# Moving the ternary quantisation of a weight into the last batch of a kernel's first half, and reordering the transfers at the change of halves

## The chip, the cores and the metric

The kernel runs on one core of one Trainium2 chip. The metric is the device time of one execution in microseconds (us); the median over several executions counts. The engines are called TensorE (PE in the profile; PEld is its weight load), VectorE (DVE), ScalarE (ACT), GpSimd (POOL) and SyncE (SP, which here issues every DMA transfer, in the order of its program).

## What is computed

The input x has 8 batches of 1024 tokens by 512 channels, fp32. Each token row is layer-normalised to xn, and the output is x + attention(xn) + ffn(xn).

```python
# attention, per batch
xm  = x * time_mix + shifted(x) * (1 - time_mix)
k   = exp(min(xm @ Wk.T, 60)); v = xm @ Wv.T; r = xm @ Wr.T
# per channel, along the tokens: a decaying sum of k*v and of k (a scan)
rwkv = sigmoid(r) * wkv / sum_k
out_attention = rwkv @ Wo.T
# feed-forward
xn2   = layernorm(x) * ln_gamma + ln_beta
beta  = mean(|weight|)                       # one number for the whole weight
w_q   = clip(round(weight / (beta + eps)), -1, 1)     # ternary
gamma = max(|xn2|)                           # one number over all 8 batches
y     = (clip(xn2 * 128 / gamma) @ w_q) * (gamma * beta / 128)
```

Because gamma is a maximum over all batches, the feed-forward product can't start before every batch has been normalised once. The ternary weight w_q depends on the weight alone.

## The kernel before

**Two halves.** Batches 0 to 3 form the first half (phase A in the code), batches 4 to 7 the second (phase B). In phase A a batch b gets its attention, and at the same time the feed-forward inputs of batch b and of batch b + 4 are normalised, transposed on TensorE, evacuated by ScalarE, searched for their absolute maximum by VectorE and stored to DRAM (`ffn_input`). The attention result of a phase-A batch is stored to `attn_scratch`. In phase B a batch b gets its attention, its own feed-forward product and that of batch b - 4, whose stored attention result is read back into the tile `parked`.

**The groups.** A batch has two token tiles of 512 tokens (0 and 1), and each tile has four chunks of 128 channels: eight chunks c. Every chunk has three projections, k, v and r, so a batch runs over 24 groups g = 3c + m (m = 0, 1, 2 for k, v, r). Each group on TensorE is 12 matmuls (a split of fp32 into a high and a low part, three products for each of four input chunks), `project`, L467. In phase A each group also has one transposition slot n = g (`slot`, L454), in the order of `SLOT_KINDS` (L44): 0 to 3 ffn_own0, 4 to 7 ffn_other0, 8 to 11 mix_own1, 12 to 15 ffn_own1, 16 to 19 ffn_other1, 20 to 23 mix_next0. All slots share one PSUM bank: the transposes of slot n wait until ScalarE has evacuated slot n - 1 (L456). The attention output of tile 0, 48 matmuls, runs after group 12, and that of tile 1 after group 23 (`attn_out`, L488). In phase B the feed-forward products (32 matmuls each, `ffn_out`, L508) stand behind groups 4, 9, 16 and 21.

**The order on each engine is written out by hand.** Every engine works through its own program in order and waits on semaphores; a wait holds everything behind it. For the last batch of phase A (b = 3) the steps that matter are these.

- VectorE, `batch` (L979), at g = 12 (m = 0, c = 4): `clamp_k`, `denominator`, `rwkv`, `rwkv_lo` of chunk 3, then `tile_stats("other1")` (L1018), then `add_out("attn0")` (L1019, four adds from the PSUM banks to the x tile). At g = 13: the absolute maximum of slot 13 (L859) and `recurrence` of chunk 4 (L918: the product k*v at L923, which frees the bank for the next v projection, two scans, and the sum L940). At g = 14 and 15 the maxima of slots 14 and 15, at g = 16 that of slot 16 and `tile_stats("next0")`. After the last group come `ternary_sum` (L896, the sum of |weight| by partition), `quantise` (L901), `scales` (L1050) and `add_out("attn1")`.
- ScalarE, `batch` (L717): at g = 14 it evacuates slot 14, normalises two of the four 128-token blocks of the tile `other` and takes `exp_r(4)`; at g = 15 it evacuates slot 15 (L590), then `exp_k(5)` and `ln_sums(4)` (L696, which needs VectorE's sum of chunk 4); at g = 16 it evacuates slot 16, once plain into `parked` (L589) and once scaled (L590). After the last group it waits for VectorE's rounding and writes the four chunks of `w_ternary` (L756 to L759).
- GpSimd, `batch_a` (L1159): statistics arithmetic and half of each normalisation. `other(b, "other1")` (L1167, the helper is at L1138) starts when VectorE's statistics of `other1` are ready (L1144) and ends with the row `mix_over_ffn_stat` (L1156); then comes `mix_scale` for next0. After the batch come the sum over partitions (L1198, `partition_all_reduce`), for which VectorE waits in `quantise` (L902), and the maximum over partitions (L1200), for which VectorE waits in `scales` (L1052).
- SyncE, `batch_a` (L328) with `is_last`: at the end it waits for all stores from `parked`, loads the weight into `parked` (L354), then the feed-forward input of other0 in four chunks into the tile `other` (L359), stores x[1] to scratch (L361), loads the next x[1] (L363); behind that come the mix input (L422, a 1 MB load into `normed` and a broadcast row), the load of `parked` (L424) and, at the head of `batch_b`, the four chunks of own0 (L375, the issue is at L371).

In phase B, ScalarE evacuates a chunk of `other` once it has landed (L594) and so frees it for the next load; its evacuation of own0 chunk 0 stands at g = 4, in front of `exp_r(1)` and what follows. The tile `parked` is the same memory as `PLAIN` (L115): slots 4 to 7 and 16 to 19 of phase A write it, and the weight is loaded into it.

Of the kernel before, what the change touches and what calls it, by code (L numbers as in the profile page):

```python
# [24 lines left out]
ALU = mybir.AluOpType  # L25
ACT = mybir.ActivationFunctionType
AX = mybir.AxisListType

P = 128
# [3 lines left out]
FFN_EPS = 1e-5  # L33
# [29 lines left out]
def mixed_decay_kernel(nc, x, constants, weights, Wf, out):  # L63
# [19 lines left out]
    with ExitStack() as ctx:  # L83
# [208 lines left out]
        def _(sp):  # L292
# [35 lines left out]
            def batch_a(b, is_last=False):  # L328
# [4 lines left out]
                store_ffn_input(b, 7)  # L333
                store_row(b, 0)
                store_ffn_input(b, 12)

# [12 lines left out]
                if is_last:  # L349

                    for r in range(RING):
                        sp.wait_ge(s_fst[r], 16 * 2 * HALF)
                        sp.wait_ge(s_plain[r], 16 * 2 * HALF)
                    sp.dma_start(ZB[:, :, :], Wf.rearrange("(i p) c -> p i c", p=P)).then_inc(s_w[4], 16)  # L354
                    for t in range(2):
                        sp.wait_ge(s_inv[t], 16 * HALF + 16)
                    sp.wait_ge(pe_t, slots_before(b, "A", first_slot("ffn_other1") + CH))
                    for ch in range(CH):
                        sp.dma_start(ZA[:, ch, :], ffn_in[0, 0, ch]).then_inc(s_fld[ch], 16)  # L359
                sp.wait_ge(dve_out, BANKS + bank_use(b, "A", "attn1") + Q)  # L360
                sp.dma_start(scratch_t[b, 1], X[1][:, :, :]).then_inc(s_xst[1], 16)  # L361
                sp.wait_ge(s_xst[1], 16 * b + 16)
                sp.dma_start(X[1][:, :, :], x_t[b + 1, 1]).then_inc(s_x[1], 16)  # L363

            def load_ffn_input(b, what, ch):
# [7 lines left out]
            def batch_b(b, is_last=False):  # L373
                for ch in range(CH):
                    load_ffn_input(b, "own0", ch)  # L375
                sp.wait_ge(dve_out, BANKS + bank_use(b, "B", "other0") + Q)
# [43 lines left out]

            sp.wait_ge(pe_t, slots_before(HALF - 1, "A", len(SLOTS)))
            load_mix_input(HALF, 1)  # L422
            sp.wait_ge(act_q, CH)
            sp.dma_start(ZB[:, :, :], scratch_t[0, 0]).then_inc(s_park, 16)  # L424
            for b in range(HALF, B - 1):
# [131 lines left out]
        def _(act):  # L557
# [145 lines left out]
            def rwkv_hi(b, ph, c):  # L703
# [11 lines left out]
                nc.scalar.activation(RH[:, j, :], KV[:, c % 2, 1, :], ACT.Copy).then_inc(act_rh, 1)  # L715

            def batch(b, ph, is_last=False, last_a=False):  # L717
                last = None
                for g in range(GROUPS):
# [21 lines left out]
                    elif m == 2:  # L741
                        if c and c != CH:
                            rwkv_hi(b, ph, c - 1)
                        if g == ATTN0_AFTER - 1:
                            high_part(b, ph, last)
                            last = None
                            if ph == "A":
                                normalise(b, ph, "ffn_own1")
                        exp_r(b, c)
                ln_sums(b, CHUNKS - 1)  # L750
                if last is not None:
                    high_part(b, ph, last)
                quotient(b, CHUNKS - 1)
                rwkv_hi(b, ph, CHUNKS - 1)
                if last_a:
                    act.wait_ge(dve_q, 3)  # L756
                    for i in range(CH):
                        nc.scalar.activation(WQ[:, i, :], ZB[:, i, :], ACT.Sign,
                                             bias=round_c[:, :]).then_inc(act_q, 1)  # L759
                elif ph == "A":  # L760
                    normalise(b + 1, ph, "ffn_own0")
# [12 lines left out]
        def _(dve):  # L774
# [126 lines left out]
            def quantise():  # L901
                dve.wait_ge(pool_sum, 1)  # L902
                V.tensor_scalar(sc[:, 2:3], sc[:, 1:2], 1.0 / (C * C), None, ALU.mult).then_inc(dve_s, 1)
                dve.wait_ge(dve_s, 2)
                V.tensor_scalar(sc[:, 3:4], sc[:, 2:3], FFN_EPS, None, ALU.add).then_inc(dve_s, 1)
                dve.wait_ge(dve_s, 3)
                V.reciprocal(sc[:, 4:5], sc[:, 3:4]).then_inc(dve_q, 1)
# [71 lines left out]
            def batch(b, ph, is_last=False, last_a=False):  # L979
                last = None  # L980
                for g in range(GROUPS):
# [28 lines left out]
                    if m == 0:  # L1010
                        clamp_k(b, c)
                        if c:
                            denominator(b, c - 1)
                            if c == CH:
                                rwkv(b, c - 1)
                                rwkv_lo(b, c - 1)
                                if ph == "A":
                                    tile_stats(b, ph, "other1", is_last)  # L1018
                                add_out(b, ph, "attn0")  # L1019
                    elif m == 1:  # L1020
# [13 lines left out]
                if last_a:  # L1034
                    ternary_sum()
                    quantise()
                    scales()
# [34 lines left out]
        def _(pool):  # L1072
# [86 lines left out]
            def batch_a(b, is_last=False):  # L1159
# [6 lines left out]
                normalise(XN, X[1], own[:, 1], 1, pool_xn)  # L1166
                other(b, "other1")  # L1167
                mix_scale(*mix_call(b, "A", "next0"), own[:, 0])
                pool.wait_ge(pe_t, slots_before(b, "A", first_slot("ffn_own1") + CH))
# [26 lines left out]
            batch_a(HALF - 1, is_last=True)  # L1196
            pool.wait_ge(dve_q, 1)
            G.partition_all_reduce(sc[:, 1:2], sc[:, 0:1], P, bass.bass_isa.ReduceOp.add).then_inc(pool_sum, 1)  # L1198
            pool.wait_ge(dve_s, 1)
            G.partition_all_reduce(sc[:, 6:7], sc[:, 5:6], P, bass.bass_isa.ReduceOp.max).then_inc(pool_max, 1)  # L1200
# [36 lines left out]
```

## Time and profile before

| quantity | value |
|---|---|
| time, median of 3 runs | 922.42 us (918.77, 922.57, 922.42) |
| time of the profiled execution | 919.68 us |
| its span | 917.9 us |
| mean granted TensorE clock | 0.992 |
| TensorE busy | 880.4 us, 96% |
| VectorE busy | 761.5 us, 83% |
| ScalarE busy | 509.4 us, 56% |
| GpSimd busy | 188.1 us, 20% |
| phase B starts on TensorE | 440.9 us from the start of the span |

The profiled execution takes 1.8 us more than its span. The times below are microseconds from the span's start. In a timeline a row gives start, duration, engine, source line, operation, tile written and tiles read, the shape, and how many instructions it merges; what stands in brackets is the engine's idle time before it and who ended it. Durations of neighbours on one engine overlap a little, so the step from one to the next is shorter than a duration: a matmul row shows about 0.4 us and the next begins 0.23 us later.

### The profile page before, as it was taken

The page shows a single profiled execution, that of the slowest core. Times are in us where ns is not written, and L with a number is a line of the kernel's source. Part 1 is how long each engine was busy: PE and PEld are TensorE (multiplying, and loading weights), DVE is VectorE, ACT ScalarE, POOL GpSimd, SP SyncE. Part 2 cuts the span into 40 slices and gives each one's busy share as a digit, 9 for nine tenths or more (in the row PEclk, how much of TensorE's full clock was granted, in tenths as well). Part 3 has the DMA queues.
Part 4 walks back from the last instruction along what each step waited for, and adds up shares of the span by engine and source line. Part 5 has one row for each costly group of instructions (what it writes and reads, how often), then busy time and mean ns, then how long its engine had stood idle before and what let it go on. Part 6 is the DMA issues. An engine that isn't in the chain of part 4 may idle for free.

```text
span 917.9 us, 12736 instructions
## 1 busy us (share of the span) xinstructions
PE 880.4 (96%) x3984; PEld 714.3 (78%) x3984; DVE 761.5 (83%) x1282; ACT 509.4 (56%) x830; POOL 188.1 (20%) x242
## 2 busy tenths in 40 slices
PE   2989999999999999999989999999999999999998
PEld 2768777787878777787867888888888888888886
DVE  5998988889798988889768887887878978789684
ACT  3674757657574757657445363554545544455441
POOL 5442333143242333140010020100201102011000
PEclk9999999999999999999999999999999999999999
DMA  8222415042422415043425443253332532334211
GB/s 275 105 81 80 150 41 186 15 149 69 149 80 77 152 46 181 14 151 112 154 97 185 138 144 111 80 192 137 110 115 107 194 137 92 104 137 138 92 47 46
DMA packets 59841, 107.13 MB, mean 117 GB/s; under 512 B 7712, under 2 KB 7712, under 8 KB 59808
## 3 DMA queue, kind: packets, MB, share of 16 engines
q1 hardware_dynamic: 59808, 106.73, 34.2%
q8 instruction: 16, 0.26, 0.1%
q14 instruction: 17, 0.14, 0.0%
HBM read 64.76 MB, written 41.96 MB: 116 GB/s over the span
## 4 chain that ended last, share of the span: by engine, by line
PE 63%; DVE 18%; issue 9%; ACT 4%; DMA 4%; POOL 1%; SPq 0%; DVEq 0%; ACTq 0%; POOLq 0%
PE kvr L483 12%; PE kvr L485 12%; PE kvr L484 12%; PE out_banks L519 6%; PE out_banks L521 6%; PE out_banks L498 5%; PE out_banks L501 5%; PE out_banks L500 5%; DVE scans L933 4%; DVE bn_stats L796 3%; PE transposed L441 2%; DMA other<-ffn_input 1%; DVE rwkv_lo L953 1%; DVE k_and_kv L923 1%; DVE k_and_kv L949 1%
## 5 line engine op out<-in xcount | busy, mean ns | idle before, releaser
L483 PE MATMUL kvr<-xm_hi,wk_hi 128*128 128x512 f32 x256 | 104.4, 408 | 7.2 <-DVE xm_lo L876 4.6
L1186 POOL TENSOR_TENSOR evacuated<-normed,mix_over_ffn_row 128x512 f32<-128x512 f32 x28 | 36.3, 1296 | 360.0 <-DVE ffn_lo L876 360.0
L483 PE MATMUL kvr<-xm_hi,wv_hi 128*128 128x512 f32 x256 | 102.9, 402 | 1.6 <-DVE k_and_kv L923 1.1
L483 PE MATMUL kvr<-xm_hi,wr_hi 128*128 128x512 f32 x256 | 103.3, 404 | 0.0
L498 PE MATMUL out_banks<-wo_hi,rwkv_hi 128*128 128x512 f32 x256 | 101.9, 398 | 0.5 <-DVE rwkv_lo L953 0.5
L485 PE MATMUL kvr<-xm_hi,wk_lo 128*128 128x512 f32 x256 | 101.5, 396 | 0.0
L501 PE MATMUL out_banks<-wo_hi,rwkv_lo 128*128 128x512 f32 x256 | 101.3, 396 | 0.0
L500 PE MATMUL out_banks<-wo_lo,rwkv_hi 128*128 128x512 f32 x256 | 101.2, 395 | 0.0
L519 PE MATMUL out_banks<-w_ternary,ffn_hi 128*128 128x512 f32 x256 | 100.0, 390 | 1.3 <-DVE ffn_lo L876 1.3
L484 PE MATMUL kvr<-xm_lo,wk_hi 128*128 128x512 f32 x256 | 100.9, 394 | 0.0
L485 PE MATMUL kvr<-xm_hi,wr_lo 128*128 128x512 f32 x256 | 100.4, 392 | 0.0
L485 PE MATMUL kvr<-xm_hi,wv_lo 128*128 128x512 f32 x256 | 100.1, 391 | 0.0
L484 PE MATMUL kvr<-xm_lo,wr_hi 128*128 128x512 f32 x256 | 100.0, 391 | 0.0
L521 PE MATMUL out_banks<-w_ternary,ffn_lo 128*128 128x512 f32 x256 | 99.7, 390 | 0.0
L484 PE MATMUL kvr<-xm_lo,wv_hi 128*128 128x512 f32 x256 | 99.7, 389 | 0.0
L689 ACT ACTIVATE gate<-kvr 128x512 f32<-128x512 f32 x64 | 37.8, 591 | 88.8 <-PE kvr L485 88.8
L940 DVE SCALAR_TENSOR_TENSOR k_and_kv<-k_and_kv,constants,scans 128x1024 f32<-128x1024 f32 x64 | 83.4, 1303 | 1.1
L933 DVE TENSOR_TENSOR_SCAN scans<-constants,state,k_and_kv 128x512 f32<-128x512 f32 x64 | 79.7, 1287 | 0.0
L590 ACT ACTIVATE evacuated<-transposed,constants 128x512 f32<-128x512 f32 x64 | 49.6, 774 | 50.9 <-PE transposed L441 47.3
L933 DVE TENSOR_TENSOR_SCAN scans<-constants,k_and_kv 128x512 f32<-128x512 f32 x64 | 75.1, 1215 | 0.0
L627 ACT ACTIVATE ffn_hi<-evacuated 128x512 fp32r<-128x512 f32 x64 | 39.9, 623 | 50.7 <-DVE evacuated L862 48.4
L876 DVE TENSOR_TENSOR ffn_lo<-evacuated,ffn_hi 128x512 fp32r<-128x512 f32 x64 | 44.0, 687 | 25.4 <-ACT ffn_hi L627 25.1
(125 smaller groups left out, 1910.7 us busy)
## 6 DMA issues: line engine op xcount, KB each, us to landing
other<-ffn_input SPq DMA_DIRECT2D x64, 256.0 KB, 5.4
x<-in_x SPq DMA_DIRECT2D x15, 1024.0 KB, 5.7
other<-in_x SPq DMA_DIRECT2D x8, 1024.0 KB, 5.7
ffn_input<-evacuated SPq DMA_DIRECT2D x32, 256.0 KB, 4.6
ffn_input<-parked SPq DMA_DIRECT2D x32, 256.0 KB, 2.1
attn_scratch<-x SPq DMA_DIRECT2D x8, 1024.0 KB, 4.3
parked<-attn_scratch SPq DMA_DIRECT2D x8, 1024.0 KB, 7.1
out<-parked SPq DMA_DIRECT2D x8, 1024.0 KB, 5.2
```

Of the source, the lines that this page charges most:

```text
L483: nc.tensor.matmul(KVR[:, m, :], hi, XH[t][:, ch, :], start=(ch == 0), stop=False)
L484: nc.tensor.matmul(KVR[:, m, :], hi, XL[t][:, ch, :], start=False, stop=False)
L485: last = nc.tensor.matmul(KVR[:, m, :], lo, XH[t][:, ch, :], start=False, stop=(ch == CH - 1))
L498: nc.tensor.matmul(OUT[:, q, :], hi, WH["o"][:, j, :], start=(j == 0 and ph == "A"), stop=False)
L500: nc.tensor.matmul(OUT[:, q, :], hi, WL["o"][:, j, :], start=False, stop=False)
L501: last = nc.tensor.matmul(OUT[:, q, :], lo, WH["o"][:, j, :], start=False, stop=(j == CH - 1))
L519: nc.tensor.matmul(OUT[:, q, :], AH[:, ch, q * P:(q + 1) * P], WQ[:, ch, :], start=(ch == 0), stop=False)
L521: last = nc.tensor.matmul(OUT[:, q, :], AL[:, ch, q * P:(q + 1) * P], WQ[:, ch, :], start=False, stop=(not own_tile and ch == CH - 1))
L590: nc.scalar.activation(U[:, r, :], bank, ACT.Identity, bias=bet[:, ch:ch + 1], scale=gam[:, ch:ch + 1]).then_inc(act_u, 1)
L876: V.tensor_tensor(lo, U[:, n % RING, :], hi.bitcast(F32), ALU.subtract).then_inc(dve_lo, 1)
L933: last = V.tensor_tensor_scan(S[:, i, 1:TILE + 1], dec, kv[:, i, :], 0.0 if t == 0 else state[:, j, i:i + 1], ALU.mult, ALU.add)
L940: V.scalar_tensor_tensor(kv, kv, first[:, j:j + 1], S[:, :, 0:TILE], ALU.mult, ALU.add).then_inc(dve_sum, 1)
```

## The change

The load of the feed-forward weight moves from the end of SyncE's last phase-A batch to just behind `store_row(b, 0)`. `ternary_sum` and `quantise` on VectorE move from the end of that batch to g = 12, between `tile_stats("other1")` and `add_out("attn0")`; `scales` stays. GpSimd's sum over partitions moves to just behind `other(b, "other1")`; its maximum over partitions stays behind the batch. ScalarE's four ternary chunks move to the ends of g = 14 and g = 15, two each. On SyncE the load of `parked` goes ahead of other0's chunks, the mix input ahead of the store of x[1], and own0's four chunks ahead of the load of the next x[1]. The counts of the semaphore `dve_s` are renumbered to the new order.

```diff
--- before.py
+++ after.py
@@ -332,6 +332,11 @@
                 sp.dma_start(ZA[:, :, :], x_t[b + HALF, 1]).then_inc(s_oth, 16)
                 store_ffn_input(b, 7)
                 store_row(b, 0)
+                if is_last:
+
+                    for ch in range(CH):
+                        sp.wait_ge(s_plain[ch], 16 * (2 * b + 1))
+                    sp.dma_start(ZB[:, :, :], Wf.rearrange("(i p) c -> p i c", p=P)).then_inc(s_w[4], 16)
                 store_ffn_input(b, 12)
 
                 sp.wait_ge(dve_out, BANKS + bank_use(b, "A", "attn0") + Q)
@@ -351,16 +356,26 @@
                     for r in range(RING):
                         sp.wait_ge(s_fst[r], 16 * 2 * HALF)
                         sp.wait_ge(s_plain[r], 16 * 2 * HALF)
-                    sp.dma_start(ZB[:, :, :], Wf.rearrange("(i p) c -> p i c", p=P)).then_inc(s_w[4], 16)
+                    load_parked()
                     for t in range(2):
                         sp.wait_ge(s_inv[t], 16 * HALF + 16)
                     sp.wait_ge(pe_t, slots_before(b, "A", first_slot("ffn_other1") + CH))
                     for ch in range(CH):
                         sp.dma_start(ZA[:, ch, :], ffn_in[0, 0, ch]).then_inc(s_fld[ch], 16)
+                    sp.wait_ge(pe_t, slots_before(b, "A", len(SLOTS)))
+                    load_mix_input(HALF, 1)
                 sp.wait_ge(dve_out, BANKS + bank_use(b, "A", "attn1") + Q)
                 sp.dma_start(scratch_t[b, 1], X[1][:, :, :]).then_inc(s_xst[1], 16)
+                if is_last:
+
+                    for ch in range(CH):
+                        load_ffn_input(HALF, "own0", ch)
                 sp.wait_ge(s_xst[1], 16 * b + 16)
                 sp.dma_start(X[1][:, :, :], x_t[b + 1, 1]).then_inc(s_x[1], 16)
+
+            def load_parked():
+                sp.wait_ge(act_q, CH)
+                sp.dma_start(ZB[:, :, :], scratch_t[0, 0]).then_inc(s_park, 16)
 
             def load_ffn_input(b, what, ch):
 
@@ -371,8 +386,9 @@
                 sp.dma_start(ZA[:, ch, :], ffn_in[bb, int(what[-1]), ch]).then_inc(s_fld[ch], 16)
 
             def batch_b(b, is_last=False):
-                for ch in range(CH):
-                    load_ffn_input(b, "own0", ch)
+                if b > HALF:
+                    for ch in range(CH):
+                        load_ffn_input(b, "own0", ch)
                 sp.wait_ge(dve_out, BANKS + bank_use(b, "B", "other0") + Q)
                 sp.dma_start(out_t[b - HALF, 0], ZB[:, :, :]).then_inc(s_parkst, 16)
                 for ch in range(CH):
@@ -418,10 +434,6 @@
                 batch_a(b)
             batch_a(HALF - 1, is_last=True)
 
-            sp.wait_ge(pe_t, slots_before(HALF - 1, "A", len(SLOTS)))
-            load_mix_input(HALF, 1)
-            sp.wait_ge(act_q, CH)
-            sp.dma_start(ZB[:, :, :], scratch_t[0, 0]).then_inc(s_park, 16)
             for b in range(HALF, B - 1):
                 batch_b(b)
             batch_b(B - 1, is_last=True)
@@ -713,6 +725,14 @@
                     if ph == "B":
                         act.wait_ge(pe_out, bank_use(b, ph, "other0"))
                 nc.scalar.activation(RH[:, j, :], KV[:, c % 2, 1, :], ACT.Copy).then_inc(act_rh, 1)
+
+            TERNARY_AT = {14: (0, 1), 15: (2, 3)}
+
+            def ternary(chunks):
+
+                act.wait_ge(dve_q, 3)
+                for i in chunks:
+                    nc.scalar.activation(WQ[:, i, :], ZB[:, i, :], ACT.Sign, bias=round_c[:, :]).then_inc(act_q, 1)
 
             def batch(b, ph, is_last=False, last_a=False):
                 last = None
@@ -747,17 +767,14 @@
                             if ph == "A":
                                 normalise(b, ph, "ffn_own1")
                         exp_r(b, c)
+                    if last_a and g in TERNARY_AT:
+                        ternary(TERNARY_AT[g])
                 ln_sums(b, CHUNKS - 1)
                 if last is not None:
                     high_part(b, ph, last)
                 quotient(b, CHUNKS - 1)
                 rwkv_hi(b, ph, CHUNKS - 1)
-                if last_a:
-                    act.wait_ge(dve_q, 3)
-                    for i in range(CH):
-                        nc.scalar.activation(WQ[:, i, :], ZB[:, i, :], ACT.Sign,
-                                             bias=round_c[:, :]).then_inc(act_q, 1)
-                elif ph == "A":
+                if ph == "A" and not last_a:
                     normalise(b + 1, ph, "ffn_own0")
 
             with act.Fori(0, HALF - 1) as b:
@@ -901,9 +918,9 @@
             def quantise():
                 dve.wait_ge(pool_sum, 1)
                 V.tensor_scalar(sc[:, 2:3], sc[:, 1:2], 1.0 / (C * C), None, ALU.mult).then_inc(dve_s, 1)
+                dve.wait_ge(dve_s, 1)
+                V.tensor_scalar(sc[:, 3:4], sc[:, 2:3], FFN_EPS, None, ALU.add).then_inc(dve_s, 1)
                 dve.wait_ge(dve_s, 2)
-                V.tensor_scalar(sc[:, 3:4], sc[:, 2:3], FFN_EPS, None, ALU.add).then_inc(dve_s, 1)
-                dve.wait_ge(dve_s, 3)
                 V.reciprocal(sc[:, 4:5], sc[:, 3:4]).then_inc(dve_q, 1)
                 dve.wait_ge(dve_q, 2)
                 V.tensor_scalar(ZB[:, :, :], ZB[:, :, :], sc[:, 4:5], ROUND, ALU.mult, ALU.add).then_inc(dve_q, 1)
@@ -1016,6 +1033,9 @@
                                 rwkv_lo(b, c - 1)
                                 if ph == "A":
                                     tile_stats(b, ph, "other1", is_last)
+                                if last_a:
+                                    ternary_sum()
+                                    quantise()
                                 add_out(b, ph, "attn0")
                     elif m == 1:
                         if c and c != CH:
@@ -1032,8 +1052,6 @@
                     tile_stats(b + 1, ph, "other0", is_last)
                     largest(b)
                 if last_a:
-                    ternary_sum()
-                    quantise()
                     scales()
                 add_out(b, ph, "attn1")
 
@@ -1165,6 +1183,9 @@
                 pool.wait_ge(pe_t, slots_before(b, "A", first_slot("mix_own1") + CH))
                 normalise(XN, X[1], own[:, 1], 1, pool_xn)
                 other(b, "other1")
+                if is_last:
+                    pool.wait_ge(dve_q, 1)
+                    G.partition_all_reduce(sc[:, 1:2], sc[:, 0:1], P, bass.bass_isa.ReduceOp.add).then_inc(pool_sum, 1)
                 mix_scale(*mix_call(b, "A", "next0"), own[:, 0])
                 pool.wait_ge(pe_t, slots_before(b, "A", first_slot("ffn_own1") + CH))
                 normalise(XN, X[0], own[:, 0], 0, pool_xn)
@@ -1194,9 +1215,7 @@
             with pool.Fori(0, HALF - 1) as b:
                 batch_a(b)
             batch_a(HALF - 1, is_last=True)
-            pool.wait_ge(dve_q, 1)
-            G.partition_all_reduce(sc[:, 1:2], sc[:, 0:1], P, bass.bass_isa.ReduceOp.add).then_inc(pool_sum, 1)
-            pool.wait_ge(dve_s, 1)
+            pool.wait_ge(dve_s, 3)
             G.partition_all_reduce(sc[:, 6:7], sc[:, 5:6], P, bass.bass_isa.ReduceOp.max).then_inc(pool_max, 1)
             with pool.Fori(HALF, B - 1) as b:
                 batch_b(b)
```

## Rows read from the trace of the kernel before

**Rows 1.** the page, part 1: busy time, share of the span, instructions

```profile
PE 880.4 (96%) x3984; PEld 714.3 (78%) x3984; DVE 761.5 (83%) x1282; ACT 509.4 (56%) x830; POOL 188.1 (20%) x242
```

**Rows 2.** timeline of TensorE: start, duration (us), instruction, tiles, count

```profile
440.93 0.39 PE L483 MATMUL kvr<-xm_hi,wk_hi 128*128 128x512 f32 x1
...
497.49 0.39 PE L498 MATMUL out_banks<-wo_hi,rwkv_hi 128*128 128x512 f32 x1
...
564.32 0.39 PE L483 MATMUL kvr<-xm_hi,wk_hi 128*128 128x512 f32 x1
...
614.19 0.39 PE L498 MATMUL out_banks<-wo_hi,rwkv_hi 128*128 128x512 f32 x1
```

**Rows 3.** timeline of TensorE, 476 us; in brackets idle time and who ended it

```profile
476.00 0.50 PE L483 MATMUL kvr<-xm_hi,wk_hi 128*128 128x512 f32 x1 [2.63 <-ACT k_and_kv L685]
```

**Rows 4.** busy time by stretch; PEclk is the granted TensorE clock, 1.00 full

```profile
core 0: us, PE busy (x) PEld busy (x) DVE busy (x) ACT busy (x) POOL busy (x), PEclk, DMA share, GB/s
...
477.40:480.70 3.30, 3.30 (x10) 2.53 (x9) 3.30 (x7) 2.35 (x4) 1.29 (x1) 0.50 0.00 0
```

**Rows 5.** timeline around the change of halves: SyncE's queue, then ScalarE

```profile
452.10 3.26 SPq L371 DMA_DIRECT2D other<-ffn_input  x4
...
464.85 0.81 ACT L599 ACTIVATE evacuated<-other,beta_beta,gamma_beta 128x512 f32<-128x512 f32 x1 [8.21 <-DMA other<-ffn_input]
```

**Rows 6.** timeline of VectorE, end of the last batch of the first half

```profile
437.89 2.28 DVE L898 TENSOR_REDUCE scalars<-parked 128x1 f32<-128x2048 f32 x1
440.75 0.15 DVE L903 TENSOR_SCALAR scalars<-scalars 128x1 f32<-128x1 f32 x1 [0.57 <-POOL scalars L1198]
...
442.53 0.15 DVE L1053 SCALAR_TENSOR_TENSOR scalars<-scalars 128x1 f32<-128x1 f32 x1
```

**Rows 7.** timeline of ScalarE, the ternary weights

```profile
442.65 2.56 ACT L758 ACTIVATE w_ternary<-parked,minus_round 128x512 fp32r<-128x512 f32 x4 [5.39 <-DVE parked L909]
```

**Rows 8.** timeline of GpSimd, last batch of the first half

```profile
392.43 0.20 POOL L1146 TENSOR_SCALAR stat_work<-mean_var 128x4 f32<-128x4 f32 x1 [14.28 <-DVE mean_var L801]
...
400.14 0.39 POOL L1156 TENSOR_TENSOR mix_over_ffn_stat<-stat_work 128x4 f32<-128x4 f32 x1 [0.18 <-POOLq L1157]
...
440.31 0.40 POOL L1198 PARTITION_ALL_REDUCE scalars<-scalars  x1 [25.42 <-DVE scalars L898]
```

**Rows 9.** instructions of lines 1079, 1198, 1186: count, min/median/max ns, first and last start

```profile
L1079 POOLq MODIFY_POOL_CONFIG  x2: 11/11/11, 1.3 to 1.3; - x2
L1079 POOL TENSOR_SCALAR_AFFINE_SELECT ident<-ident x1: 292/292/292, 1.4 to 1.4; 128x128 f32<-128x128 f32 x1
...
L1198 POOLq MODIFY_POOL_CONFIG  x2: 8/8/8, 414.8 to 414.9; - x2
...
L1186 POOL TENSOR_TENSOR evacuated<-normed,mix_over_ffn_row x28: 1286/1297/1304, 472.5 to 836.0; 128x512 f32<-128x512 f32 x28
L1186 POOLq MODIFY_POOL_CONFIG  x6: 11/11/11, 460.2 to 668.7; - x6
```

**Rows 10.** timeline of VectorE, middle of the last batch of the first half

```profile
392.15 2.45 DVE L971 TENSOR_TENSOR x<-x,out_banks 128x512 f32<-128x512 f32 x4
...
396.02 0.69 DVE L923 TENSOR_TENSOR k_and_kv<-k_and_kv,kvr 128x512 f32<-128x512 f32 x1 [0.83 <-PE kvr L485]
...
400.39 0.68 DVE L859 TENSOR_REDUCE absmax<-evacuated 128x1 f32<-128x512 f32 x1
...
404.82 0.69 DVE L859 TENSOR_REDUCE absmax<-evacuated 128x1 f32<-128x512 f32 x1 [0.46 <-ACT evacuated L590]
```

**Rows 11.** timeline of ScalarE, the same stretch

```profile
400.47 0.76 ACT L590 ACTIVATE evacuated<-transposed,constants 128x512 f32<-128x512 f32 x1
...
402.92 0.71 ACT L696 ACTIVATE k_and_kv<-k_and_kv,k_eps 128x512 f32<-128x512 f32 x1
403.53 0.59 ACT L589 ACTIVATE parked<-transposed 128x512 f32<-128x512 f32 x1
```

**Rows 12.** timeline of TensorE, the same stretch

```profile
402.22 0.60 PE L441 MATMUL transposed<-ident,other 128*128 128x128 f32 x4
```

## Prediction

> **What bounds the kernel now.** I read the page first: TensorE is busy 96% of the span [rows 1], so only time in which it stands still or runs slowly can be won, and any new standstill is lost. Next I compared two like stretches of TensorE's timeline. From the first k projection of a phase-B batch to its first attention-output matmul the work is the same in every batch. In the first phase-B batch it takes 497.49 - 440.93 = 56.56 us, in a later one 614.19 - 564.32 = 49.87 us [rows 2]. So the change of halves costs TensorE 6.7 us, and that is all that can be won there. Of this, 2.63 us is one wait for ScalarE's exp of k [rows 3]. From 477.4 to 480.7 us the granted clock was 0.50, that is 1.2 instead of 2.4 GHz, where it had been full before that wait [rows 4]. The reader should look for what ended last behind this. The four loads of own0 were issued from 452.10 us on, behind five transfers of x, the mix input and `parked`. ScalarE stood 8.21 us for the first of them, until 464.85 [rows 5], with exp_r(1) and all later work of its program behind it.
>
> The ternary work itself costs TensorE almost nothing before: VectorE spends 442.53 - 437.89 = 4.6 us on sum and rounding [rows 6] and ScalarE 2.56 us [rows 7], but TensorE already runs projections of phase B, from 440.93 us on, without a gap.
>
> **The change part by part.**
>
> *The transfers.* The own0 loads now wait only for other0's evacuations and go out beside a single 1 MB store. I expect the first to land well before ScalarE asks for it, and take the full 6.7 us as gain; the lower end is 0, if another wait takes the place. The weight load moves to a quiet place: `parked` is free once other0's four stores have landed, SyncE's next item comes many microseconds later, and VectorE asks for the weight only at 392 us. `parked` from scratch and the mix input go out earlier, each well ahead of its reader. The load of x[1] falls behind four own0 issues, but x[1] is first touched at the end of that batch. I cost all of these at 0.
>
> *The sum over partitions.* This is where I expect the loss. At g = 12 VectorE now sums |weight| behind the statistics of other1. The statistics end where the adds of attn0 began, 392.15 us [rows 10], and the sum takes 2.28 us [rows 6], so it is done at 394.4. Then VectorE waits for GpSimd. But GpSimd has just been released by these same statistics and works through `other1` from 392.43 to 400.14 + 0.39 = 400.53 us [rows 8]; its sum over partitions stands behind that.
>
> *The configuration of GpSimd.* Before its sum over partitions GpSimd runs two MODIFY_POOL_CONFIG, at 414.8 us, and before the first ordinary multiply of phase B again, at 460.2 [rows 9]. In the kernel before, both had room behind them: the first 25.42 us of idleness [rows 8], the second 472.5 - 460.2 = 12.3 us [rows 9]. In the changed kernel the pair stands directly between 400.53 and a sum for which VectorE waits. Call its price L. Lower end: 0, since at the start of the kernel an operation followed its pair within 0.1 us [rows 9], though that pair need not have changed anything. Upper end: 12.3 us, since the multiply at 472.5 was released by VectorE and ran at once. No row decides between them; neither end is a real switch with nothing to hide it, so I take the middle, L = 6.1 us.
>
> The Trainium skill (GPSIMD Engine Reference, section Instruction dispatch) says that the first call into a freshly loaded kernel pays a load of about 6 us (5.95 us, counted from MODIFY_POOL_CONFIG) that the profile doesn't show. That rule speaks against this change; no row here shows such a load uncovered. With 5.95 instead of 6.1 us the sum would be 0.15 us less.
>
> *The sum for VectorE.* Sum over partitions and its signal: 0.57 us [rows 6], so VectorE goes on at 400.53 + 0.57 + L = 401.1 + L. Scalars and rounding take 442.53 - 440.75 = 1.78 us [rows 6]: 402.9 + L. The four adds (about 2.4) and one maximum (about 0.6) [rows 10] come next, so k*v of chunk 4 starts at 405.9 + L, against 396.02 before [rows 10].
>
> *The sum for ScalarE.* From that product to the maximum of slot 14, directly behind the chunk's sum, is 400.39 - 396.02 = 4.37 us [rows 10]: ln_sums(4) can start at 410.3 + L. It takes 403.53 - 402.92 = 0.6 us [rows 11]. Then two ternary chunks, half of 2.56 us = 1.3 [rows 7]. Then the two evacuations of slot 16, after which VectorE's maximum of slot 16 started 404.82 - 403.53 = 1.3 us later [rows 10, 11]. That maximum starts at 413.5 + L, against 404.82: a lag of **8.7 + L** us, 14.8 with L = 6.1.
>
> *What of it reaches TensorE.* All of it, I think. Slot 16 is transposed only when slot 15 is evacuated, which ScalarE does behind the first two ternary chunks, at 402.9 + L + 1.3 + 0.7 = 404.9 + L. TensorE was there at 402.22 [rows 12], so it stands 2.7 + L = 8.8 us. Then the v projection waits for k*v until 406.6 + L, and slot 17 for the evacuation of slot 16. Behind that, VectorE's order runs nearly gapless to the end of the batch and TensorE is close behind it, so neither catches up, and in phase B TensorE has no gaps in which lost time could be hidden. A long standstill may lower the clock again: in the one case shown, TensorE worked at half speed for 3.3 us behind a wait [rows 3, 4] and so lost half of that, 1.6 us. I take one such stretch, with ends at 0 (it falls into the standstill) and 3.2 (two).
>
> *At the end of the half.* VectorE and ScalarE are rid of 4.6 and 2.6 us there. TensorE didn't wait for them, so this gives nothing beyond the 6.7 us. GpSimd's switch back to ordinary operations starts at 401.1 + L and is first asked for after the maximum of slot 16, at 413.5 + L plus statistics: over 12 us of cover. The third switch, ahead of the maximum over partitions, has the 25 us that cover it now [rows 8].
>
> **The sum.** 14.8 + 1.6 - 6.7 = **+9.7 us**. Against the profiled execution (919.68 us: 917.9 of span and 1.8 around it) that gives 929.4. The median of the runs shown stands 2.7 above that execution, but the mean of all four times shown is 920.9; I take that as the base: **930.6 us**. A measurement of this kernel can tell about 0.5%, 4.6 us, from no change.
>
> **The rivals.**
>
> *A, the switch costs nothing* (L = 0, the code is resident). For it: the pair at the start that cost 0.1 us; against it: the pair's being there. Even so VectorE waits from 394.4 to 401.1 us for GpSimd's `other1`, and the sum is 8.7 + 0 to 1.6 - 6.7 = +2 to +3.6: about 923.5, no change that can be told. Chance 0.14.
>
> *B, the switch costs as much as the trace leaves room for*, 12.3 us: 21.0 + 1.6 - 6.7 = +15.9, 936.8. Chance 0.07.
>
> *C, the change of halves is not mended*: own0 is on time, but something behind it (the exp chain, x[1], the mix input) holds TensorE as long. Then 14.8 + 1.6 = +16.4, 937.3. Against it: in later phase-B batches the same code has no gap [rows 2]. Chance 0.10.
>
> *D, faster.* VectorE's wait for GpSimd stays off TensorE's path, because TensorE has transposes and projections queued ahead until slot 16. The only gain of 6.7 us is then left: 914.2. It decides at slot 16: TensorE is there at 402.22 us, so the rounding would have to be done by about 400.2, which is before GpSimd has even finished `other1`. So it also needs GpSimd to be much quicker beside an idle VectorE. Chance 0.04.
>
> **How the numbers follow.** My forecast has 0.65. The predicted time is that of the forecast, 930.6. The range reaches from rival A's 923.5 to L of about 12 or rival C, 937.5: **923.5 to 937.5**; it holds the forecast's own spread (clock 0 to 3.2 us, base 2 us either way, GpSimd perhaps 1 us quicker). Faster by over 0.5%: 0.04 (D). Within 0.5%: A and the lowest part of the forecast, 0.16. Slower by over 0.5%: 0.80.
>
> **What would show each step.** In the changed kernel's profile:
> - GpSimd: MODIFY_POOL_CONFIG near 400.6 us, and the sum over partitions L later; if it starts within 1 us, A is right. If it starts near 407, the forecast is.
> - VectorE: a wait for GpSimd of 6.7 + L, near 13 us, in front of the line that scales the sum.
> - ScalarE: a wait of several us in front of the first ternary chunk; TensorE: waits for ScalarE's evacuation ahead of slot 16 (about 9 us) and slot 17, and one for k*v between them, with a granted clock of 0.50 in a stretch near them.
> - The first k projection of phase B starts at 440.93 + 16.4, about 457 us, and the stretch from it to the first attention output is 49.9 us, without ScalarE's wait for own0.
>
> I am wrong if the last A batch shows waits of TensorE under 5 us in total, or if the stretch of the first phase-B batch stays above 53 us.

## The result, and the profile after

| | before | changed |
|---|---|---|
| median | 920.67 us (918.77 to 922.57, 4 runs) | 934.33 us (933.76 to 934.40, 4 runs) |
| profiled execution | 919.68 us, span 917.9 | 934.32 us, span 932.5 |

The ratio is 1.0152, with a 95% interval of 1.013 to 1.0175: slower by 1.5%, 13.7 us. The forecast was 930.6 with a range of 923.5 to 937.5.

The page's head and its first part say only that the same work lies in a longer span (compare [rows 1]):

```profile
span 932.5 us, 12742 instructions
...
PE 883.2 (95%) x3984; PEld 717.0 (77%) x3984; DVE 761.2 (82%) x1282; ACT 509.6 (55%) x830; POOL 181.7 (19%) x242
```

Two stretches of TensorE's timeline say where the time went. I time the first from the v projection of chunk 4 in the last batch of the first half (right behind the point where the ternary work now sits) to the first k projection of the second half: 440.93 - 392.99 = 47.94 us before, 462.25 - 393.47 = 68.78 after, so **20.8 us lost**. The second runs from there to the first attention output of the second half: 56.56 us before [rows 2], and after the change, by TensorE's timeline,

```profile
462.25 0.39 PE L495 MATMUL kvr<-xm_hi,wk_hi 128*128 128x512 f32 x1
```

```profile
512.13 0.39 PE L510 MATMUL out_banks<-wo_hi,rwkv_hi 128*128 128x512 f32 x1
```

512.13 - 462.25 = 49.88 us, which is the length of a later batch, so **6.7 us won**. The difference, 14.2, and the 0.5 us by which this execution was already later at the v projection make the 14.6 us between the spans.

**GpSimd** (instructions by line: count, min/median/max ns, first and last start). Line 1188 is the moved sum over partitions, line 1111 the first ordinary operation of `mix_scale`:

```profile
L1188 POOLq MODIFY_POOL_CONFIG  x2: 11/11/11, 399.7 to 399.8; - x2
L1188 POOL PARTITION_ALL_REDUCE scalars<-scalars x1: 401/401/401, 405.4 to 405.4; - x1
```

```profile
L1111 POOLq MODIFY_POOL_CONFIG  x2: 11/11/11, 423.7 to 423.7; - x2
```

From the pair at 399.8 us to the sum at 405.4 there are 5.7 us in which GpSimd had nothing to wait for: VectorE's part had been ready since 394.9. The second pair stands at 423.7, not behind the sum. GpSimd's timeline shows what came of it:

```profile
430.46 0.19 POOL L1111 TENSOR_SCALAR stat_work<-mean_var 128x4 f32<-128x4 f32 x1 [24.62 <-issue]
...
432.33 0.20 POOL L1114 TENSOR_TENSOR own_stats<-stat_work,own_stats 128x4 f32<-128x4 f32 x1 [0.18 <-POOL own_stats L1113]
```

The arithmetic for next0 starts 6.7 us behind the pair. In the kernel before, the same line (there L1093) started 0.2 us behind the statistics:

```profile
408.62 0.43 POOL L1093 TENSOR_SCALAR stat_work<-mean_var 128x4 f32<-128x4 f32 x1 [8.09 <-DVE mean_var L801]
```

**VectorE** (timeline; compare [rows 10]):

```profile
392.62 2.25 DVE L915 TENSOR_REDUCE scalars<-parked 128x1 f32<-128x2048 f32 x1
405.87 0.15 DVE L920 TENSOR_SCALAR scalars<-scalars 128x1 f32<-128x1 f32 x1 [11.00 <-POOL scalars L1188]
...
407.65 2.47 DVE L988 TENSOR_TENSOR x<-x,out_banks 128x512 f32<-128x512 f32 x4
...
410.64 0.68 DVE L940 TENSOR_TENSOR k_and_kv<-k_and_kv,kvr 128x512 f32<-128x512 f32 x1
...
418.24 0.69 DVE L876 TENSOR_REDUCE absmax<-evacuated 128x1 f32<-128x512 f32 x1 [1.04 <-ACT evacuated L602]
420.44 2.47 DVE L813 BATCH_NORM_STATS2 bn_stats<-x 128x6 f32<-128x512 f32 x4 [1.52 <-DMA x<-in_x]
```

The reader should see one wait of 11.00 us for GpSimd at 405.87 (forecast 6.7 + 5.7 = 12.4), then the chain of the prediction: adds at 407.65 (forecast 402.9 + 5.7 = 408.6), k*v at 410.64 (411.6), the maximum of slot 16 at 418.24 (419.2), each about 1 us early. GpSimd's `other1` was quicker than in the kernel before: it ran from 392.90 to 399.80, 6.9 us, against 8.1 us in [rows 8]. A small wait that I had not listed follows at 420.44: 1.52 us for the next x[0]. Its load stands behind the store of x[0], and that behind the delayed adds. In the kernel before, these statistics followed without a gap at 405.42.

**ScalarE** (timeline; compare [rows 11]):

```profile
407.77 1.33 ACT L735 ACTIVATE w_ternary<-parked,minus_round 128x512 fp32r<-128x512 f32 x2 [6.71 <-DVE parked L926]
409.01 0.76 ACT L602 ACTIVATE evacuated<-transposed,constants 128x512 f32<-128x512 f32 x1
...
415.74 1.32 ACT L735 ACTIVATE w_ternary<-parked,minus_round 128x512 fp32r<-128x512 f32 x2
...
424.06 0.63 ACT L727 ACTIVATE rwkv_hi<-k_and_kv 128x512 fp32r<-128x512 f32 x1 [3.84 <-DVE k_and_kv L966]
...
432.56 1.52 ACT L654 ACTIVATE normed<-x,own_stats 128x512 f32<-128x512 f32 x2 [5.48 <-POOL own_stats L1114]
```

It waits 6.71 us for the rounding, 3.84 us for a product of VectorE that stands behind the late statistics of next0, and 5.48 us for `own_stats`, which is the second switch.

**TensorE** (timeline, the waits ahead of slots 16, 17, 19 and 20; what ended them is ScalarE's evacuation each time):

```profile
410.01 1.09 PE L453 MATMUL transposed<-ident,other 128*128 128x128 f32 x4 [7.16 <-ACT evacuated L602]
```

```profile
418.26 0.66 PE L453 MATMUL transposed<-ident,other 128*128 128x128 f32 x4 [1.57 <-ACT evacuated L602]
```

```profile
427.14 0.66 PE L453 MATMUL transposed<-ident,other 128*128 128x128 f32 x4 [2.29 <-ACT evacuated L602]
```

```profile
436.56 1.08 PE L453 MATMUL transposed<-ident,normed 128*128 128x128 f32 x4 [6.00 <-ACT evacuated L602]
```

Each names ScalarE. Behind ScalarE stand the rounding (slot 16), VectorE's sum of the chunk (17), its product behind the statistics of next0 (19) and GpSimd's switch (20). The granted clock fell during the two long ones (busy time by stretch):

```profile
core 0: us, PE busy (x) PEld busy (x) DVE busy (x) ACT busy (x) POOL busy (x), PEclk, DMA share, GB/s
406.20:416.20 10.00, 5.82 (x15) 4.51 (x16) 9.89 (x16) 3.57 (x6) 0.00 (x0) 0.50 0.42 136
433.50:440.10 6.60, 3.54 (x11) 2.99 (x12) 4.87 (x8) 5.12 (x9) 0.88 (x2) 0.50 0.17 41
442.00:450.00 8.00, 8.00 (x41) 6.60 (x40) 6.56 (x17) 7.36 (x14) 0.43 (x1) 1.00 0.60 98
```

There were two stretches at 0.50 (1.2 GHz). In the first TensorE stood still nearly half the time and its one projection would have had to wait for slot 17 anyway. In the second, the projection behind slot 20 took 4.3 us (437.30 to 441.63 in the timeline) where its like takes 3.0. Behind the wait of 2.29 us at slot 19 the projection ran at full speed.

**SyncE at the change of halves** (timeline; compare [rows 5]):

```profile
463.16 0.37 SPq L368 DMA_DIRECT2D attn_scratch<-x  x1
463.58 11.51 SPq L386 DMA_DIRECT2D other<-ffn_input  x4
475.13 0.43 SPq L374 DMA_DIRECT2D x<-in_x  x1
```

own0's first chunk goes out 0.4 us behind the store, ahead of x[1]. ScalarE never waits for it.

### The profile page after: what moved, and what is told of

Its sections match the earlier page's. It is cut to its first block, busy times and chain, and to the rows that moved or that the text cites. A ratio compares the mean times of both kernels' runs of the same rounds, so it can differ in the third digit from the quotient of the medians.

```text
span 932.5 us, 12742 instructions
## 1 busy us (share of the span) xinstructions
PE 883.2 (95%) x3984; PEld 717.0 (77%) x3984; DVE 761.2 (82%) x1282; ACT 509.6 (55%) x830; POOL 181.7 (19%) x242
## 4 chain that ended last, share of the span: by engine, by line
PE 68%; DVE 16%; issue 7%; ACT 5%; DMA 2%; POOL 1%; SPq 0%; DVEq 0%; ACTq 0%; POOLq 0%
PE kvr L495 13%; PE kvr L497 13%; PE kvr L496 13%; PE out_banks L533 6%; PE out_banks L531 6%; PE out_banks L510 5%; PE out_banks L513 5%; PE out_banks L512 5%; DVE scans L950 3%; DVE bn_stats L813 3%; PE transposed L453 2%; DVE rwkv_lo L970 1%; DVE k_and_kv L940 1%; DVE absmax L876 1%; DVE k_and_kv L966 1%
## 5 line engine op out<-in xcount | busy, mean ns | idle before, releaser
L453 PE MATMUL transposed<-ident,normed 128*128 128x128 f32 x260 | 41.5, 284 | 25.9 <-ACT evacuated L602 11.6
```

The source lines that it names most:

```text
L453: last = nc.tensor.transpose(bank[:, q * P:(q + 1) * P], src[:, q, ch * P:(ch + 1) * P], ident[:, :])
```

## Experiments

The two stretches of TensorE's timeline, in us, and the medians. The kernel before ran beside each group on the same chip: 919.90 us beside e1 to e4, 919.76 beside e5 to e7.

| kernel | v of chunk 4 to second half | first batch to attention output | median | ratio to before (95%) |
|---|---|---|---|---|
| before | 47.94 | 56.56 | | |
| changed | 68.78 | 49.88 | 934.33 | 1.0152 (1.013 to 1.0175) |
| e1 transfers alone | 47.95 | 49.90 | 912.82 | 0.9923 (0.991 to 0.9935) |
| e2 ternary alone | 68.77 | 51.20 | 934.98 | 1.0167 (1.0152 to 1.0182) |
| e3 switch back early | 62.42 | 49.87 | 927.38 | 1.0085 (1.0068 to 1.0103) |
| e4 no switch | 56.66 | 49.88 | 921.62 | 1.0022 (1.0013 to 1.0032) |
| e5 no switch, ahead of other1 | 51.85 | 49.88 | 916.70 | 0.9965 (0.9953 to 0.9976) |
| e6 own0 alone ahead | 47.95 | 54.06 | 917.93 | 0.9974 (0.9964 to 0.9985) |
| e7 sum one group earlier | 49.19 | 49.88 | 917.06 | 0.9969 (0.9959 to 0.9979) |

**e1, the transfers alone**, on the kernel before:

```diff
                 sp.dma_start(scratch_t[b, 1], X[1][:, :, :]).then_inc(s_xst[1], 16)
+                if is_last:
+                    load_ffn_input(HALF, "own0", 0)
+                    sp.wait_ge(act_q, CH)
+                    sp.dma_start(ZB[:, :, :], scratch_t[0, 0]).then_inc(s_park, 16)
+                    for ch in range(1, CH):
+                        load_ffn_input(HALF, "own0", ch)
                 sp.wait_ge(s_xst[1], 16 * b + 16)
```

The mix input goes ahead of this store, as in the change.

> The kernel before with the new order of transfers alone: own0's chunks ahead of the next x[1], mix input ahead of the store of x[1], parked between own0's first and second chunk (it must wait for the ternary chunks, which stay at the end of the half). Theory 1 (late own0 loads cost the 6.7 us at the change of halves, the ternary work at the end of the half costs nothing): 6 to 7 us less than before, about 914, and 49.9 us from the first k projection of the second half to its first attention output. Rival (the ternary work at the end of the half is what makes the first batch of the second half slow): no change, about 920.7, and that stretch stays at 56 us.

Measured: 912.82 us, 7.1 less than before, and 49.90 us for the first batch. SyncE's timeline:

```profile
446.79 0.37 SPq L363 DMA_DIRECT2D attn_scratch<-x  x1
447.20 0.51 SPq L379 DMA_DIRECT2D other<-ffn_input  x1
447.75 1.01 SPq L367 DMA_DIRECT2D parked<-attn_scratch  x1
448.98 7.57 SPq L379 DMA_DIRECT2D other<-ffn_input  x3
456.59 0.43 SPq L371 DMA_DIRECT2D x<-in_x  x1
```

The whole gain at the change of halves is there with the ternary work still at the end of the half. So the transfers are enough for it. This kernel is faster than both the kernel before and the changed one.

**e2, the ternary work alone**: the changed kernel with the old order of `parked`, mix input, x[1] and own0.

> The changed kernel with the old order of transfers at the change of halves (the early weight load stays, it is needed). Theory 1: the whole lag of the last batch of the first half, 21.3 us, and the late own0 loads again: 20 to 22 us more than before, about 941 to 943. Rival (the gain comes from taking the ternary work away from the end of the half): like the changed kernel, about 934.

Measured: 934.98 us. The lag is that of the changed kernel, 68.77, but the first batch lost only 51.20 - 49.88 = 1.3 us, not 6.7. My expectation missed by 6 to 8 us, and the rival's number was right. ScalarE's wait for own0 is still there, but shorter than the 8.21 us of [rows 5]:

```profile
480.00 0.82 ACT L606 ACTIVATE evacuated<-other,beta_beta,gamma_beta 128x512 f32<-128x512 f32 x1 [4.46 <-DMA other<-ffn_input]
```

SyncE's timeline shows why. First the store of x[1] in the kernel before, then e2 from that store on:

```profile
445.61 0.37 SPq L361 DMA_DIRECT2D attn_scratch<-x  x1
```

```profile
462.35 0.37 SPq L365 DMA_DIRECT2D attn_scratch<-x  x1
...
468.85 5.42 SPq L379 DMA_DIRECT2D other<-ffn_input  x4
```

The store of x[1] was issued 462.35 - 461.44 = 0.9 us after the first k projection of the second half, against 445.61 - 440.93 = 4.7 us in the kernel before, because VectorE's adds of attn1 no longer stand behind the ternary work. The four transfers behind it, and own0 behind those, move with it: own0 is issued 468.85 - 461.44 = 7.4 us after that projection, against 452.10 - 440.93 = 11.2 [rows 5]. So own0 was late for two reasons in a row. Either move alone takes most of the 6.7 us (the transfers 6.7, the ternary work 5.4), and the two don't add up.

**e3, the switch back at once**:

```diff
                     G.partition_all_reduce(sc[:, 1:2], sc[:, 0:1], P, ...).then_inc(pool_sum, 1)
+                    G.tensor_scalar(touch[:, :], half_pos[:, 0:1], 1.0, 0.0, ALU.mult, ALU.add)
```

> The changed kernel with one small ordinary GpSimd operation on one number per partition straight behind the sum over partitions, so that GpSimd switches back to ordinary operations there and not behind its wait for the statistics of next0. Theory 1 (the switch back costs 6.7 us of TensorE's time because it stands behind that wait): 6 to 8 us less than the changed kernel, about 927, and ScalarE's wait of 5.5 us for own_stats is gone. Rival (the lag is the ternary work itself in a full stretch, the switch back lies beside it): no change, about 934.

Measured: 927.38, 6.9 us less than the changed kernel. The second pair now runs right behind the sum over partitions (instructions of the line of `touch`):

```profile
L1190 POOLq MODIFY_POOL_CONFIG  x2: 83/83/83, 405.2 to 405.3; - x2
```

In its waits from 400 to 470 us (engine, tile and line that waited, and whom for: total us, times, longest) the second switch lies under VectorE's own work:

```profile
DVE scalars L921 <- POOL scalars L1189: 10.8, 1, 10.8
...
POOL touch L1190 <- issue: 7.0, 1, 7.0
...
POOL scalars L1189 <- issue: 5.4, 1, 5.4
```

Nobody waits for `touch`, and 68.78 - 62.42 = **6.4 us** of TensorE's time came back. That is standstill alone: TensorE's waits between slots 16 and 20 add up to 17.4 us in the changed kernel and to 11.1 here. A stretch at half speed is still there, behind the 2.40 us wait at slot 19; the projection that starts with this row needed 4.3 us:

```profile
427.48 0.78 PE L496 MATMUL kvr<-xm_hi,wv_hi 128*128 128x512 f32 x1
```

**e4, no switch**: the sum over partitions is replaced by an ordinary operation in the same place. The kernel leaves that sum out and so works with a wrong beta; its other instructions and waits are those of the changed kernel.

```diff
-                    G.partition_all_reduce(sc[:, 1:2], sc[:, 0:1], P, ...).then_inc(pool_sum, 1)
+                    G.tensor_scalar(sc[:, 1:2], sc[:, 0:1], 128.0, 0.0, ALU.mult, ALU.add).then_inc(pool_sum, 1)
```

> The changed kernel with the sum over partitions left out: an ordinary GpSimd operation multiplies each partition's own sum by 128 instead, so that there is no switch in the last batch of the first half. All other instructions and waits stay. Theory 1 (both switches are exposed, 5.7 and 6.7 us, with a half-speed stretch behind them): 12 to 14 us less than the changed kernel, about 921 to 922; what is left of the lag is GpSimd's other1 and the ternary work itself, 8 us, against a gain of 6.7. Rival (the ternary work in a full stretch is the loss): 930 or more.

Measured: 921.62. The waits from 390 to 430 us:

```profile
DVE scalars L920 <- POOL scalars L1188: 5.1, 1, 5.1
...
PE transposed L453 <- ACT evacuated L602: 4.8, 4, 2.3
```

Against e3, another 62.42 - 56.66 = **5.8 us**: the first switch. What stays is 56.66 - 47.94 = 8.7 us. Of this, 5.2 us are longer waits of TensorE (6.3 us in the stretch against 1.1 before); the rest is time at half speed, which the trace shows from 403.9 to 407.2 and from 410.7 to 414.2 us. VectorE still waits 5.1 us for GpSimd, now for `other1` alone.

**e5, as e4, ahead of `other1`**:

```diff
-                other(b, "other1")
                 if is_last:
                     pool.wait_ge(dve_q, 1)
                     G.tensor_scalar(sc[:, 1:2], sc[:, 0:1], 128.0, ...).then_inc(pool_sum, 1)
+                other(b, "other1")
```

> As e4 (the sum over partitions left out, each partition's own sum times 128 instead, so no switch), and this operation stands ahead of other1 in GpSimd's program, not behind it. Theory 1 (of the 8.7 us of lag that e4 kept, GpSimd's other1, 6 us after VectorE's sum, is the larger part, and the ternary work itself costs 2 to 3 us): 4 to 6 us less than e4, 916 to 917.5, and about 50.5 us instead of 56.7 from the v projection of chunk 4 to the first k projection of the second half. Rival (VectorE and ScalarE are so full there that their 4 and 2.6 us of ternary work are the lag, wherever the sum comes from): within 2 us of e4, 920 to 921.6.

Measured: 916.70, and 51.85 us, so 56.66 - 51.85 = **4.8 us** for `other1` and 51.85 - 47.94 = **3.9 us** for the ternary work. That last part was more than the 2 to 3 expected: 2.5 us are longer waits, and about 1.4 us come from one projection at half speed, from 416.32 us on, behind the longest of them. TensorE's waits for ScalarE's evacuations are down to (390 to 450 us)

```profile
PE transposed L453 <- ACT evacuated L602: 3.7, 3, 2.3
```

**e6, own0 alone ahead**: on the kernel before, own0's chunks go ahead of x[1], while the mix input and `parked` stay behind.

> The kernel before with one change of order: own0's four chunks ahead of the load of the next x[1]; the mix input and parked stay behind it. Theory 1 (own0 alone was late): as e1, 913 to 914. Rival (the mix input and parked are then late in its place, since they are issued some 10 us later than before): 916 to 920, and the trace shows VectorE waiting for parked or GpSimd for the mix input.

Measured: 917.93, and 54.06 us for the first batch: 2.5 of 6.7 us. The rival was right. The waits from 440 to 505 us:

```profile
DVE parked L975 <- DMA parked<-attn_scratch: 4.9, 1, 4.9
...
PE out_banks L523 <- DVE ffn_lo L880: 2.6, 1, 2.6
...
PE out_banks L523 <- DVE parked L975: 0.8, 1, 0.8
```

`parked` came late in own0's place: it was issued at 457.02 us, against 451.44 in the kernel before (I had expected 10 us later, it was 5.6). VectorE stood 4.9 us for it, and TensorE behind VectorE. So own0's place alone isn't enough, and `parked` has to move too. Whether the mix input had to move was not tried alone.

**e7, the sum one group earlier**: `ternary_sum` at g = 11; on GpSimd the sum over partitions and `touch` ahead of `other1`.

```diff
                         rwkv_lo(b, c - 1)
+                        if last_a:
+                            ternary_sum()
...
                                 if last_a:
-                                    ternary_sum()
                                     quantise()
```

> The changed kernel with VectorE's sum of the weight one group earlier (g = 11), GpSimd's sum over partitions ahead of other1, where GpSimd was idle for 14 us, and the small ordinary operation straight behind it, so that both switches lie in that idle time. The result is that of the reference. Theory 1 (both switches and other1 are off the path, only the ternary work is left in it, 2 to 3 us, against the gain of 6.7): 915 to 918. Rival (two switches of 5.7 and 6.4 us plus the sum don't fit into the idle time and delay other1): 920 or more, and GpSimd's first operation of other1 comes some us behind the statistics.

Measured: 917.06. This kernel leaves nothing out. GpSimd's timeline:

```profile
383.18 0.40 POOL L1189 PARTITION_ALL_REDUCE scalars<-scalars  x1 [5.63 <-DVE scalars L916]
390.75 0.62 POOL L1190 TENSOR_SCALAR touch<-half 128x1 f32<-128x1 f32 x1 [7.17 <-issue]
394.43 0.20 POOL L1166 TENSOR_SCALAR stat_work<-mean_var 128x4 f32<-128x4 f32 x1 [3.06 <-DVE mean_var L819]
```

The sum and both switches fit into the idle time, and GpSimd even waits for the statistics at 394.43. The idle time in front of 390.75 is the switch back again. What is left is the ternary work itself:

```profile
PE out_banks L511 <- DVE rwkv_lo L971: 2.0, 1, 2.0
...
PE transposed L454 <- ACT evacuated L603: 1.4, 3, 0.7
```

TensorE waits 2.0 us for the last chunk of rwkv_lo, in the attention output of tile 0 and so ahead of the stretch that I time, and then runs at half speed until about 395 us. From the start of that attention output to the v projection of chunk 4 it takes 396.17 - 380.76 = 15.4 us, against 392.99 - 381.36 = 11.6 in the kernel before: 3.8 us. The stretch that I time is 49.19 - 47.94 = 1.3 us longer. Together that is a loss of 5.0 us, more than the 3.9 of e5, which doesn't have the first part. So the idea of the change can be made to work: by the medians e7 is 2.7 us faster than the kernel before. But e1 is better by another 4 us, since it leaves the ternary work at the end of the half, where with the new order of transfers it costs TensorE nothing.

## Why the prediction was right, and where a step of it failed

The sign and the range were right; the forecast change of 9.7 us was 4 us short of the 13.7 measured.

- **The lag of 8.7 + L.** I had worked it out for the maximum of slot 16, and there it was too long. Counted from the v projection of chunk 4, that maximum came after 404.82 - 392.99 = 11.8 us before, after 410.87 - 391.98 = 18.9 in e4 and after 418.24 - 393.47 = 24.8 in the changed kernel. So the lag was 7.1 without a switch and 12.9 with it, 1.5 to 1.6 less than 8.7 and 8.7 + 5.7. Most of this is GpSimd's quicker `other1`, 1.2 us. Behind slot 16 the lag grew again, by VectorE's wait for x[0] (1.55 us in e4) and by TensorE's time at half speed, which I had not counted in it. That e4 loses just 8.7 us of TensorE's time in all is luck: two errors that cancel.
- **The first switch, L = 6.1.** 5.7 us between the pair and the sum in the profile, and 5.8 us of TensorE's time between e3 and e4. That the middle of two ends far apart was so good is luck; the Trainium skill (GPSIMD Engine Reference, section Instruction dispatch) has 5.95 us, and the changed kernel's trace agrees within 0.3.
- **The failed step: "GpSimd's switch back to ordinary operations starts at 401.1 + L ... over 12 us of cover."** It doesn't start there. The pair runs in front of the first ordinary operation, and in `mix_scale` the wait for the statistics of next0, which the program separates from that operation by the increment of a semaphore, stands ahead of both. (Ahead of the sum over partitions nothing stands between wait and operation, and there the pair ran before the wait: 414.8 us, against 440.31 for the sum [rows 8, 9].) So the switch began at 423.7, when the statistics were there and ScalarE and TensorE were waiting for what follows. I costed it at 0; it cost 6.4 us, as e3 shows. The trace of the kernel before could have warned me: the pair of line 1186 began at 460.2 [rows 9], 20 us after the sum over partitions at 440.31 [rows 8], not right behind it.
- **The clock, 1.6 us.** There were two stretches at 1.2 GHz, not one. The first fell mostly into a standstill, and the second cost about 1.3 us. The switch back is not its cause: e3, without that wait of 6.00 us, has a second stretch as well, behind the wait at slot 19. So this time is inside the 8.7 and 5.8 us of e4 and e3, and not in the 6.4. When the clock falls stays open: behind waits of 2.3 to 2.4 us at slot 19 it was 0.50 in e3 and e5 and full in the changed kernel.
- **The gain of 6.7 us** was exact (56.56 - 49.88). But one reason for it was wrong: I wrote that the ternary work at the end of the half "costs TensorE almost nothing". Taken away alone it gives 5.4 us (e2), since it held up the transfers in front of own0. It gave nothing *beyond* the 6.7, as forecast, because the transfers had already taken it.
- **The sum again with what was measured**: 8.7 + 5.8 + 6.4 - 6.7 = 14.2 us, and the spans differ by 14.6. This sum has no separate term for the clock, so my 1.6 us covered part of the missing 6.4 by luck. The range, too, was wide enough for another reason: its upper end stood for a longer first switch or an unmended change of halves, and neither happened.

Rival A (no cost of the switch) fell with the 5.7 us; rival B with the same number; rival C with the 49.88 us; and rival D with TensorE's wait of 7.16 us at slot 16.

## What to carry to other kernels

Before moving work earlier "under" something, read what every engine in its chain is doing at the new place, and in which order: here VectorE waited 11 us for a sum of 0.4 us, because GpSimd was released by the same event for other work first and then had to change its configuration. On GpSimd, count each change between a sum over partitions and ordinary operations as a switch in both directions, and place the way back by hand, ahead of the next wait. And where a standstill has two causes in a row, removing either can take most of it, as here: cost them together, and keep the cheaper remedy, here the order of the transfers.

## What the runs showed of the hardware that I had not expected

The switch costs time both ways, and the way back is the longer one: 5.7 us from the pair of MODIFY_POOL_CONFIG to the sum over partitions in the changed kernel, 6.7 us from the pair to the first ordinary operation behind it, and 7.0 and 7.2 us of idle time in front of `touch` in e3 and e7. In the rows of the first switch and of `touch` GpSimd waits for nothing that the profile names ("issue"). What happens in this time no run shows.

GpSimd's `other1` took 6.9 us where VectorE stood waiting (the changed kernel and e4) and 7.9 to 8.1 us where VectorE worked beside it (the kernel before, e5 and e7).
